# Scores of a cross-attention in eight 32x64 TensorE tiles rather than two of 64x128, with all clippings first

## The reference

```
q = proj(layernorm(x), Wq, bq)        # 16 heads of 16 channels
k = proj(ctx, Wk, bk); v = proj(ctx, Wv, bv)
scores = einsum('bhsd,bhtd->bhst', q, k) / sqrt(16)
scores = clip(scores, -50, 50)
scores = where(mask, scores, -10000); scores = clip(scores, -50, 50)
probs  = softmax(scores)
delta  = layernorm(rs * (probs @ v @ Wo.T + bo)) * gamma + beta
```

## Time and profile before

| | us |
|---|---|
| median of 3 runs | 682.53 (681.33 to 1588.65) |
| the profiled execution | 685.34 |
| its span in the trace | 683.5 |
| PE busy | 654.0, 96% of the span |
| DVE, ACT, POOL busy | 428.2, 273.8, 61.7 |
| the 16 batches of X1, first scores to the last `values` | 143.57, from 414.86 to 558.43 |

### The profile page before, as it was taken

How to read it: one execution, slowest core, us unless ns; L and a number is a source line. 1 busy time by engine, 2 the same in 40 slices (tenths; PEclk the granted TensorE clock), 3 DMA queues, 4 the chain that set the end, 5 groups by cost and what they waited for, 6 DMA issues and landing times.

```text
span 683.5 us, 21600 instructions
## 1 busy us (share of the span) xinstructions
PE 654.0 (96%) x9572; PEld 428.5 (63%) x9572; DVE 428.2 (63%) x998; ACT 273.8 (40%) x502; POOL 61.7 (9%) x132
## 2 busy tenths in 40 slices
PE   9999999999988999999999999999999999999876
PEld 4665666667565566666666657667667765456654
DVE  4543557577765655555544854544878975777687
ACT  2444545445442333333335735444244454011124
POOL 1010000000000111111010013000201102000000
PEclk9999999999999999999999999999999999999999
DMA  7252111116007201110005421111294100000000
GB/s 234 62 163 64 34 33 60 37 34 218 2 3 247 94 32 33 33 32 2 1 2 169 141 61 36 61 34 33 64 243 127 36 3 1 2 3 3 3 1 32
DMA packets 42365, 42.25 MB, mean 62 GB/s; under 512 B 15904, under 2 KB 33056, under 8 KB 42016
## 3 DMA queue, kind: packets, MB, share of 16 engines
q1 hardware_dynamic: 42272, 40.86, 19.4%
HBM read 40.33 MB, written 0.52 MB: 60 GB/s over the span
## 4 chain that ended last, share of the span: by engine, by line
PE 79%; DVE 13%; issue 3%; ACT 2%; DMA 1%; SPq 1%; POOL 0%; DVEq 0%; ACTq 0%
PE psum L379 14%; PE psum L387 14%; PE psum L1127 7%; PE psum L454 5%; PE psum L429 4%; PE psum L419 4%; PE psum L1178 4%; PE psum L1133 4%; PE psum L1852 2%; PE psum L1829 2%; PE psum L404 2%; PE psum L1876 2%; PE psum L1148 2%; PE psum L1162 1%; PE psum L1833 1%
## 5 line engine op out<-in xcount | busy, mean ns | idle before, releaser
L379 PE MATMUL psum<-arena 128*128 128x512 f32 x256 | 122.9, 604 | 2.4 <-issue 1.4
L387 PE MATMUL psum<-arena 128*128 128x256 f32 x512 | 122.4, 384 | 0.2 <-ACT arena L654 0.2
L387 PEld LDWEIGHTS psum<-arena 128*128 128x128 f32 x512 | 93.4, 190 | 20.7 <-issue 8.5
L680 ACT ACTIVATE arena<-arena 128x512 f32<-128x512 f32 x64 | 48.6, 806 | 71.9 <-DVE arena L805 71.9
L379 PEld LDWEIGHTS psum<-arena 128*128 128x128 f32 x256 | 44.5, 190 | 44.2 <-issue 41.4
L454 PEld LDWEIGHTS psum<-arena 128*17 128x17 f32 x4096 | 39.3, 96 | 35.2 <-issue 30.6
L805 DVE TENSOR_SCALAR arena<-psum 128x512 f32<-128x512 f32 x64 | 40.9, 685 | 24.1 <-PE psum L419 20.9
L674 ACT ACTIVATE arena<-psum,arena 128x512 f32<-128x512 f32 x64 | 40.7, 687 | 31.0 <-DVE arena L792 30.9
L1127 PE MATMUL psum<-y_cols,arena 128*128 128x512 f32 x112 | 52.9, 605 | 0.0
L454 PE MATMUL psum<-arena 128*17 128x32 f32 x4096 | 48.6, 195 | 1.8 <-ACT arena L680 0.9
L1230 ACT ACTIVATE arena<-psum 128x512 f32<-128x512 f32 x48 | 28.5, 597 | 49.0 <-PE psum L1127 30.8
(11 more groups left out here) (248 smaller groups left out, 947.7 us busy)
## 6 DMA issues: line engine op xcount, KB each, us to landing
arena<-in_ctxT SPq DMA_DIRECT2D x32, 512.0 KB, 3.7
arena<-in_L_attn_Wv SPq DMA_DIRECT2D x1, 2048.0 KB, 8.4
arena<-in_L_attn_Wq SPq DMA_DIRECT2D x8, 256.0 KB, 2.9
arena<-in_L_attn_Wk SPq DMA_DIRECT2D x8, 256.0 KB, 3.3
arena<-in_L_attn_Wo SPq DMA_DIRECT2D x1, 2048.0 KB, 11.0
arena<-in_L_ffn_w_gating SPq DMA_DIRECT2D x1, 2048.0 KB, 7.7
arena<-in_L_attn_wo SPq DMA_DIRECT2D x2, 1024.0 KB, 5.8
arena<-in_wq_upT SPq DMA_DIRECT2D x2, 768.0 KB, 8.0
```

The costliest lines, as they stand in the source:

```text
L379: last = nc.tensor.matmul(bank, wkv[:, c, i * P:(i + 1) * P], x[:, c, :], start=(c == 0), stop=(c == NC - 1))
L387: last = nc.tensor.matmul(bank[:, kk * D:(kk + 1) * D], x[:, c, k * P:(k + 1) * P], wkv[:, c, D:2 * D], start=(c == 0), stop=(c == NC - 1))
L680: nc.scalar.activation(pTk[b % 2][k], clip[k // 2][:, k % 2, :], ACT.Exp, bias=mb[:, b, k:k + 1], scale=m01[:, b, k:k + 1]).then_inc(s_exp, 1)
```

## The change

The scores of a batch are made in one go by products of 32 partitions x 64 keys as weights (two heads by 64 keys) with 32 x 64 columns of queries: four row groups `r`, each with its own PSUM bank, and two column groups `c` of 64 PSUM partitions are the eight tiles. That is 4 x 2 x 8 = 64 products or 128 pairs a batch in place of 16 or 32 pairs. All four clips follow as DVE's first work of the batch, all four exponentials wait for all four clips, and they stand behind ACT's copy of the first unit. There is one clip buffer, read by the exponentials of a batch and written by the clips of the next. `values` 0, 1 and 2 follow one another. `separate` makes two copies of the queries rather than four.

```diff
-    def scores_cols(pe, b, kp):
-        if kp == 0:
-            pe.wait_ge(s_qbd, 2 * b + 2)
...
-        wait(pe, s_mx, 4 * b + 2 * kp - 2)
-        for kk in range(2):
-            for h in range(NC):
-                for r in range(2):
-                    k, a = 2 * kp + kk, slice(64 * r, 64 * r + 64)
-                    ins = nc.tensor.matmul(S[2 * kp + r][:, (2 * kk + h) * P:(2 * kk + h + 1) * P],
-                                           kT[home(b)][a, h, k * P:(k + 1) * P],
+    def scores_cols(pe, b):
+        pe.wait_ge(s_qbd, 2 * b + 2)
...
+        wait(pe, s_mx, 4 * b)
+        for k in range(KT):
+            for h in range(NC):
+                for c in range(2):
+                    for r in range(4):
+                        a, keys = slice(32 * r, 32 * r + 32), slice(64 * c, 64 * c + 64)
+                        ins = nc.tensor.matmul(S[r][keys, (NC * k + h) * 64:(NC * k + h + 1) * 64],
+                                               kT[home(b)][a, h, k * P + 64 * c:k * P + 64 * c + 64],
...
     def batch_cols_pe(pe, b):
-        scores_cols(pe, b, 0)
+        scores_cols(pe, b)
...
             values(pe, b - 1, 0), values(pe, b - 1, 1)
-        scores_cols(pe, b, 1)
-        if b:
             values(pe, b - 1, 2)
...
     def exp_cols(act, b, k):
-        act.wait_ge(s_mx, 4 * b + k // 2 * 2 + 2)
+        act.wait_ge(s_mx, 4 * b + 4)
...
     def batch_cols_act(act, b):
-        exp_cols(act, b, 0), exp_cols(act, b, 1)
         copy_out_cols(act, tile_at(b, OUT))
         for u in own(b, 0, 0):
             unit_act(act, u)
-        exp_cols(act, b, 2), exp_cols(act, b, 3)
+        for k in range(KT):
+            exp_cols(act, b, k)
...
-    def clip_cols(v, b, i):
-        wait(v, s_exp, 4 * b + 2 * kp - 2)
+    def clip_cols(v, b, r):
+        wait(v, s_exp, 4 * b)
...
     def batch_cols_dve(v, b):
-        clip_cols(v, b, 0), clip_cols(v, b, 1)
+        for r in range(4):
+            clip_cols(v, b, r)
         delta_add(v, tile_at(b, TAKE + 1))
         for u in own(b, 1, 0):
             unit_dve(v, u)
-        clip_cols(v, b, 2), clip_cols(v, b, 3)
```

More of the change, by code:

```diff
@@ L237, in xattn @@
     QBUFS = 2 if L0 else 3
-    SEP = 2 if L0 else HG
-    qbd = [take([P, NC, SEP, SQ]) for _ in range(QBUFS)]
+    qbd = [take([P, NC, 2, SQ]) for _ in range(QBUFS)]
     qT = take([P, NC, ROWS])
@@ L253, in xattn @@
     else:
-        clip = [take([P, 2, H * SQ]) for _ in range(2)]
+        clip = take([P, KT, H * SQ])
         pTk = [[take([P, H * SQ]) for _ in range(KT)] for _ in range(2)]
@@ L311, in separate @@
     def separate(g, b):
-        mask = e.headmask[:, HG:HG + 2] if L0 else e.headmask[:, 0:HG]
         wait(g, s_scores, 4 * (b + 1 - QBUFS))
@@ L316, in separate @@
             cols = qT[:, h, b * SQ:(b + 1) * SQ]
-            nc.gpsimd.tensor_tensor(qbd[b % QBUFS][:, h, :, :], cols.unsqueeze(1).to_broadcast([P, SEP, SQ]),
-                                    mask.unsqueeze(2).to_broadcast([P, SEP, SQ]), ALU.mult).then_inc(s_qbd, 1)
+            nc.gpsimd.tensor_tensor(qbd[b % QBUFS][:, h, :, :], cols.unsqueeze(1).to_broadcast([P, 2, SQ]),
+                                    e.headmask.unsqueeze(2).to_broadcast([P, 2, SQ]), ALU.mult).then_inc(s_qbd, 1)
     def delta_power(g, t):
@@ L406, in scores_rows @@
             ins.then_inc(s_scores, 1)
-    def scores_cols(pe, b, kp):
-        if kp == 0:
-            pe.wait_ge(s_qbd, 2 * b + 2)
-            pe.wait_ge(s_ev[0], 2 * b + 1)
-            pe.wait_ge(s_ev[1], 2 * b + 1)
-        wait(pe, s_mx, 4 * b + 2 * kp - 2)
-        for kk in range(2):
-            for h in range(NC):
-                for r in range(2):
-                    k, a = 2 * kp + kk, slice(64 * r, 64 * r + 64)
-                    ins = nc.tensor.matmul(S[2 * kp + r][:, (2 * kk + h) * P:(2 * kk + h + 1) * P],
-                                           kT[home(b)][a, h, k * P:(k + 1) * P],
-                                           qbd[b % QBUFS][a, h, :, :].rearrange("p j q -> p (j q)"), start=True, stop=True)
-                    if kk == 1 and h == NC - 1:
-                        ins.then_inc(s_scores, 1)
+    def scores_cols(pe, b):
+        pe.wait_ge(s_qbd, 2 * b + 2)
+        for h in range(NC):
+            pe.wait_ge(s_ev[h], 2 * b + 1)
+        wait(pe, s_mx, 4 * b)
+        for k in range(KT):
+            for h in range(NC):
+                for c in range(2):
[3 more added lines that the diff above has]
+                                               kT[home(b)][a, h, k * P + 64 * c:k * P + 64 * c + 64],
+                                               qbd[b % QBUFS][a, h, :, :].rearrange("p j q -> p (j q)"), start=True, stop=True)
+                        if k == KT - 1 and h == NC - 1 and c == 1:
+                            ins.then_inc(s_scores, 1)
     def turn(pe, b, g):
@@ L676, in exp_cols @@
     def exp_cols(act, b, k):
-        act.wait_ge(s_mx, 4 * b + k // 2 * 2 + 2)
+        act.wait_ge(s_mx, 4 * b + 4)
         if k == 0:
             wait(act, s_pv, 4 * (b - 1))
-        nc.scalar.activation(pTk[b % 2][k], clip[k // 2][:, k % 2, :], ACT.Exp, bias=mb[:, b, k:k + 1],
+        nc.scalar.activation(pTk[b % 2][k], clip[:, k, :], ACT.Exp, bias=mb[:, b, k:k + 1],
                              scale=m01[:, b, k:k + 1]).then_inc(s_exp, 1)
@@ L797, in copy_pT_dve @@
         nc.vector.tensor_copy(pT[g % 2].rearrange("p k q -> p (k q)"), S[g]).then_inc(s_pT_dve, 1)
-    def clip_cols(v, b, i):
-        kp, r = i // 2, i % 2
-        v.wait_ge(s_scores, 4 * b + i + 1)
-        wait(v, s_exp, 4 * b + 2 * kp - 2)
-        dst = clip[kp].rearrange("p k (h r n) -> p (k h) r n", h=NC, r=2)[:, :, r, :]
-        nc.vector.tensor_scalar(dst, S[i].rearrange("p (a n) -> p a n", n=P), 50.0, -50.0, ALU.min, ALU.max)\
+    def clip_cols(v, b, r):
+        v.wait_ge(s_scores, 4 * b + r + 1)
+        wait(v, s_exp, 4 * b)
+        dst = clip.rearrange("p k (h r n) -> p (k h) r n", h=NC, r=4)[:, :, r, :]
+        nc.vector.tensor_scalar(dst, S[r].rearrange("p (a n) -> p a n", n=64), 50.0, -50.0, ALU.min, ALU.max)\
           .then_inc(s_mx, 1)
@@ L2100, in build @@
             neghalf=neghalf[:, 0:NT], neghalf2=neghalf[:, :], ident=sb("ident", [P, P])[:, :],
-            headmask=sb("head_mask", [P, HG + 2])[:, :],
+            headmask=sb("head_mask", [P, 2])[:, :],
             s_stats=sem("norm_stats"), s_var=sem("norm_var"), s_rstd=sem("norm_rstd"), s_norm=sem("norm_rows"),
@@ L2239 @@
     a["ident"] = np.eye(P, dtype=np.float32)
-    of = lambda n: (part[:, None] // DH % n == np.arange(n)[None, :]).astype(np.float32)
-    a["headmask"] = np.concatenate([of(HG), of(2)], 1)
+    a["headmask"] = (part[:, None] // DH % 2 == np.arange(2)[None, :]).astype(np.float32)
     a["L1_ffn_w_fcT"], a["L1_ffn_w_projT"] = T(a.pop("L1_ffn_w_fc")), T(a.pop("L1_ffn_w_proj"))
```

## The result

The changed kernel is slightly slower: 686.21 us median (683.85 to 690.93, 8 runs) against 683.0 us before, ratio 1.0055, 95% interval 1.0029 to 1.008. (The 683.0 is the median of 8 runs of the kernel before, made beside it.) The forecast was 674.4 us. Of the experiments, one execution of e9_more (709.29 us) fell into a slower state of the chip and is left out of its ratio. The profiled execution took 683.85 us, the fastest of the eight; its span is 682.1.

The account below looks back on a forecast made before the run. It took PE to lead early, with DVE close behind late. Savings of 8.8 + 0.2 - 1.1 + 0.2 = 8.1 us took the median from 682.53 to 674.4 us; 8-in-10 range 665 to 683, the forecast's own 671 to 679.

Parts of the forecast that it names:

- Order: where the saving is kept: Batches 0 to 3, 5, 6, 8, 9 and 10: nothing else is late, so PE's saving is kept, 8.8 us.
- the block: A batch's new scores on PE, 128 pairs: taken as 1.25 us, 1.09 to 1.38 if eight tiles overlap.
- my count of instructions: Estimate of the new scores on PE from `values`' 0.31 us per further 32 pairs: 1.29 us for 128 pairs.
- Two of the forecast's own signs of being wrong: Scores block outside 1.09 to 1.4 us; DVE idle in batches 11 and 12; a third was clips over 0.7 us each.
- `values` 0 to 2 in one piece: PE, each batch that has `values`: the three in a row take 0.98 us.
- Batch 4 pinned by POOL: POOL's all-reduce delays batch 5's query masks, so batch 4 lasts 10.4 us whatever PE saves; 0.2 us saved.
- Batch 7: DVE's copy ends 8.5 us after batch start (S7+8.5), PE waits 2.1 us; batch 10.4 rather than 9.33, 1.1 us lost.
- Batches 11 and 12 paced by DVE: DVE's queue up to batch 12's clips sets their length: 16.1 us against 15.17 before, 0.9 us lost.
- Batch 11 to the last `values`: End of the stage: 39.1 us against 39.37 before, 0.2 us gained, PE's saving turning into waiting.
- The first (order free): Rival over the whole stage: the order costs nothing, PE's full saving is kept, 666.3 us; chance 0.21.
- The second: Rival on the scores: eight tiles overlap no more than four, 2.48 us a block, 688.3 us; chance 0.08.
- The sentence on the Trainium skill's rule: Scores at about 25 ns a pair: 3.2 us for 128 pairs, kernel some 697 us; chance 0.02 of the slow rival's 0.08.

Follow-up runs that it names:

- e9_more: Kernel before, with the products of `values` g = 3 made four times rather than once, 96 pairs a batch more: 701.73 us, ratio 1.0264.
- e4_rate: Changed kernel with batch 0's score products repeated 16 times ahead of the batches, 2048 extra pairs that nobody reads: 756.81 us (one run).
- e1_order: Kernel before with its old 64x128 tiles, but all queues in the change's new order: 681.0 us, ratio 0.9971.
- e2_four: Changed kernel with four tiles of 32 rows by 128 keys rather than eight, 64 score pairs a batch rather than 128: 682.48 us, ratio 1.0000.
- e5_half_new: Changed kernel with half of `values` left out (key tiles 2 and 3), outputs not the reference's: 679.93 us, ratio 0.9953.
- e10_rows: Changed kernel with the two column groups of a row group following each other, rather than four row groups in turn: 691.47 us, ratio 1.0143.
- e3_split: Changed kernel with scores in two pieces, key tiles 0 and 1 ahead of the first unit, 2 and 3 behind it: 694.37 us, ratio 1.0160.
- e7_fix_two: e1_order with two corrections: POOL's all-reduce one batch later, DVE's odd copy of the first unit ahead of `delta_add`: 678.84 us, ratio 0.9927.
- e8_fix_four: e2_four with the same two corrections as e7_fix_two: 678.80 us, ratio 0.9929.
- e11_fix_eight: Changed kernel with the same two corrections as e7_fix_two: 685.73 us, ratio 1.0050.

## Why the prediction was wrong

**The step that failed** is "Order: where the saving is kept", with its sentence "In batches 0 to 3, 5, 6, 8, 9 and 10 nothing else is late". PE's instructions were late, a resource that the sum did not hold: 12.3 us of issue waits in the stage, where the forecast had none. The forecast did count the pairs, but priced them by the pace of a block of 32 or 64, whose instructions were already there. A stretch that consumes 448 instructions in 4.4 us asks for 100 a microsecond; e4_rate shows 69. The average of the stage, 8,536 in 146 us or 58, is below that, which is why I would not have seen it in a mean.

The forecast's own stretches show where it went. To batch 11 it had 104.2 - 7.9 = 96.3 us, measured 102.7: about 3.0 of the 6.4 us are the block (below), 3.5 the issue waits of batches 2, 3, 8, 9 and 10; those of batches 4 and 7 (1.16 and 0.97 us) fall into batches that POOL and DVE held back anyway. From batch 11 on it had 39.1, measured 43.6: issue waits of 1.75, 1.33, 1.72 and 1.91 us, part of them in time that PE would have waited for DVE, and a lower clock in batch 13. Together that is 10.9 us of the 11.8 by which the median missed. The explanation stands on the places of the waits, all at the end of a packet, and on e1, e2, e4 and e9: old number of instructions, no waits; a third of the added instructions, 1.4 us; long stream, a wait for every packet; old tiles with the added number, slower than by their work. The size of the waits in any one batch is not settled: e5 and e10 missed, and what sets the moment at which a packet is fetched is open.

**A term mis-sized: the block**, taken as 1.25 us, bounded by 1.09 and 1.38, measured 1.52. That is 11.9 ns a pair where `values` showed 9.7 for its second 32 pairs. e3_split has half the block: 0.84 us for 64 pairs, so the second 64 of the whole block take 0.68 us, 10.6 ns each. The pace is near that of `values`, as my count of instructions had it; the fixed part is larger (0.16 us by these two numbers, 0.05 in `values`). My upper bound of 1.38 came from doubling a block of 64 pairs on other tiles. What sets either part is not shown. It cost 0.27 us a batch, some 3 us before batch 11. Two of the forecast's own signs of being wrong came true: the block outside 1.09 to 1.4 us, and DVE idle for 2.0 of the 17.7 us of batches 11 and 12.

**Right, by its own steps.**
- `values` 0 to 2 in one piece: forecast 0.98, measured 0.96.
- Batch 4 pinned by POOL: forecast 10.4, measured 10.27 and, in e2_four, 10.07; moving the all-reduce frees it.
- Batch 7: the copy behind `delta_add` done at S7+8.5 and the batch 10.4 us long; measured 10.25 in e1_order, 10.07 in e2_four and in the changed kernel, 9.06 once the copy stands first.
- Batches 11 and 12 paced by DVE, 16.1 us: 16.29 in e1_order and 15.62 in e2_four, 17.71 in the changed kernel, where issue waits of 1.75 and 1.33 us fall into them.
- Batch 11 to the last `values`, 39.1 us: 39.10 in e1_order, 39.03 in e2_four and, with the corrections on the old tiles, 39.12. With eight tiles 43.59. The claim that PE's saving turns into waiting from there on held for e1, e2 and e7, whose instructions were there; it also means that the corrections gained nothing there.

**The rivals.** The first (order free) comes true in e1_order, where the order was free, but not for its reason: DVE did bind, and the merged block paid for it. The second had the right side and the wrong mechanism: tiles do overlap (1.52 us, not 2.48). The sentence on the Trainium skill's rule (TensorE: Matmul & The Clock Gate, "Wait — 56ns, not 53.3ns?": start-to-start never below about 25 ns) would have given the right side too. It would have been right by luck. The block shows 11.9 ns a pair, so the measured pairs on separate tiles, with their instructions at hand, do not keep to the rule; 29 ns a pair in e4_rate is a pace of delivery, not of issue.

**What I could have seen.** The profile before had both the queue and its packets: 76 packets of 16 KB for PE's 19,144 loads and MATMULs. It even had a wait of this kind, outside the stage: 1.39 us at 53.58 us, at PE's record 705 = 2 x 256 + 193. And the earlier trace rows gives PE's instructions by batch: 183 + 182 in 9.33 us before; the change brings them to about 550 in 8.4.

## What to carry to other kernels

Before cutting products into smaller tiles, count PE's instructions over each stretch of a few microseconds, not only its busy time. Where small tiles make a long stream of instructions, tiles twice as wide can be faster with half the instructions (e8_fix_four, 678.8 us, against e11_fix_eight, 685.7). When PE idles for "issue" in the middle of a block, count its instructions up to there: waits that keep one distance from a multiple of 256 are waits for instructions. Ask of each engine's order what a copy that frees a PE bank stands behind, and what a long POOL operation stands in front of: two moved lines were worth more here than the new tiles.

## What the hardware showed unexpectedly

**Instructions come in packets and late.** In a long stream PE works off 256 instructions, then waits and goes on 1.25 to 1.5 us after the next packet has landed; one interval took 3.45 us at best, with no other DMA about (e4_rate). The Trainium skill (Runtime: NRT & Kernel Launch, "Instruction fetch mechanics") says that the sequencer refills in 16 KiB blocks of 256 instructions while it executes the current one, and that crossing a block is "mostly hidden". The size agrees. Hidden it is here at 38 instructions a microsecond (the stage of the kernel before), nearly so at 45 (e2_four, 1.4 us of waits) and not at 58 (the changed kernel, 12.3 us).

**A wait can cost twice.** In e5_half_new a batch with a wait of 2.5 us ran at a clock of 0.74; in e4_rate, with a wait behind every 128 pairs, the clock was 0.50 (1.2 GHz) for all 47 us of repeats that were read, so that a block of 128 pairs lasts 2.26 us rather than 1.52; and in e1_order after PE's 2.0 us of waiting for POOL:

```profile
458.84:461.10 2.26, 2.26 (x30) 2.26 (x32) 1.07 (x2) 0.00 (x0) 1.38 (x4) 0.73 0.00 0
458.84:469.97 11.13, 11.13 (x180) 7.68 (x180) 4.88 (x11) 3.79 (x6) 1.38 (x4) 0.85 0.16 49
```

PE is busy for the whole of batch 5 and still takes 11.13 us for what takes 9.49 at full clock (e7_fix_two). It does not follow every wait. In e10_rows PE waits 3.25 us in this stretch, and in the changed kernel 1.91 in the next, both at full clock:

```profile
530.34:542.20 11.86, 7.70 (x284) 5.97 (x275) 7.65 (x14) 4.13 (x8) 2.51 (x7) 1.00 0.29 92
550.57:557.99 7.42, 5.51 (x282) 4.37 (x282) 6.21 (x16) 4.31 (x11) 1.10 (x2) 1.00 0.02 6
```

What decides is not shown here. A forecast that adds a wait of 2 us on PE should count with up to 1.6 us more for the clock behind it.
